# Filler products of one pass and 512 columns, and none in the stages with experts

## The reference

```python
def _L0_attn_ref(x, w_qkv, w_proj, b_proj):      # HEADS = 16, HEAD_SIZE = 8
    q, k, v = jnp.split(x @ w_qkv, 3, axis=-1)   # each to (batch, head, token, 8)
    wei = jnp.einsum('bhqd,bhkd->bhqk', q, k) * HEAD_SIZE ** (-0.5)
    wei = jax.nn.softmax(jnp.where(causal, wei, -jnp.inf), axis=-1)
    out = jnp.einsum('bhqk,bhkd->bhqd', wei, v)  # back to (batch, token, 128)
    return out @ w_proj + b_proj

def _L0_ffn_ref(x, Wg, W1, b1, W2, b2):          # 8 experts, 128 -> 512 -> 128
    topk_logits, topk_idx = jax.lax.top_k(xt @ Wg.T, 2)
    gates = zeros.at[rows, topk_idx].add(softmax(topk_logits))
    h = gelu(jnp.einsum('th,ehi->tei', xt, W1) + b1)
    o = jnp.einsum('tei,eih->teh', h, W2) + b2
    return jnp.einsum('te,teh->th', gates, o)

xn = _layernorm(x)
x = x + attn(xn) + ffn(xn)
```

## Time and profile before

| | |
|---|---|
| time before, median of 3 executions | 870.83 us (866.7 to 873.35) |
| the profiled execution, its own time | 874.43 us |
| its span, first to last instruction | 872.7 us |
| mean granted clock of TensorE | 0.842 |
| busy: PE, DVE, ACT, POOL | 740.8, 557.2, 449.5, 283.1 us |
| chain that ended last: PE, DVE, ACT, POOL | 64%, 19%, 3%, 2% |

### The profile page before, as it was taken

One profiled execution on the slowest core, in us unless ns is written; L12 is line 12 of the kernel. 1 busy time (PEld: TensorE's weight loads), 2 busy tenths in 40 slices (PEclk: granted clock), 3 DMA queues, 4 the chain that ended last, 5 costly groups with the idle time before them and its releaser, 6 DMA issues.

```text
span 872.7 us, 15135 instructions
## 1 busy us (share of the span) xinstructions
PE 740.8 (85%) x5021; PEld 420.3 (48%) x5021; DVE 557.2 (64%) x2164; ACT 449.5 (52%) x717; POOL 283.1 (32%) x454
## 2 busy tenths in 40 slices
PE   3683779986788989888898999889998989899995
PEld 2562434432345554544555555545545555555543
DVE  4749535554576666767667666756676766667656
ACT  2212123233355566655656665646566666666663
POOL 7103841573502333323132322222242323141421
PEclk9555555567797799999799989989799999898997
DMA  6997310210239051523425250605234342430074
GB/s 154 166 154 257 116 40 13 70 47 23 68 78 273 16 159 43 148 77 103 115 71 140 57 147 18 193 29 133 86 92 118 87 118 83 142 107 5 22 180 120
DMA packets 96261, 88.74 MB, mean 102 GB/s; under 512 B 8368, under 2 KB 83672, under 8 KB 96184
## 3 DMA queue, kind: packets, MB, share of 16 engines
q1 hardware_dynamic: 91432, 78.05, 34.6%
q0 software_dynamic: 4544, 9.35, 3.3%
q10 hardware_dynamic: 208, 0.38, 0.2%
HBM read 50.18 MB, written 21.32 MB: 82 GB/s over the span
## 4 chain that ended last, share of the span: by engine, by line
PE 64%; DVE 19%; issue 4%; SPq 4%; DMA 3%; ACT 3%; POOL 2%; another core or an unknown queue 2%; DVEq 0%; ACTq 0%; POOLq 0%
PE ov L773 18%; PE aux L741 15%; PE aux L831 10%; PE aux L783 6%; DVE maxes L963 5%; DVE junk L964 3%; SPq L444 3%; PE sc L695 3%; PE aux L788 2%; DMA hid<-in_L_ffn_W 2%; PE sc L696 2%; PE sc L697 2%; DVE maxes L959 2%; DVE xrow L1017 2%
## 5 line engine op out<-in xcount | busy, mean ns | idle before, releaser
L648 ACT ACTIVATE probs<-sc 128x1024 f32<-128x1024 f32 (+3 forms) x384 | 295.4, 810 | 254.5 <-PE sc L759 241.3
L741 PE MATMUL aux<-kT,qT 32*128 32x512 f32 (+3 forms) x768 | 244.6, 483 | 79.4 <-DVE maxes L964 22.6
L561 POOL TENSOR_SCALAR_AFFINE_SELECT probs<-probs 128x256 f32<-128x256 f32 x256 | 103.8, 409 | 422.7 <-ACT probs L648 418.7
L963 DVE TENSOR_REDUCE maxes<-aux 128x1 f32<-128x128 f32 (+2 forms) x384 | 161.1, 420 | 70.9 <-PE aux L741 64.3
L959 DVE TENSOR_REDUCE maxes<-aux 128x1 f32<-128x512 f32 x256 | 163.4, 684 | 60.1 <-PE aux L741 54.3
L741 PEld LDWEIGHTS aux<-kT,qT 32*128 32x128 f32 x768 | 108.3, 205 | 193.6 <-DVE maxes L964 52.7
L773 PE MATMUL ov<-probs,v 128*32 128x512 f32 (+3 forms) x1536 | 187.9, 565 | 2.4 <-POOL probs L561 2.3
L759 PE MATMUL sc<-qT,kT 32*128 32x512 f32 (+3 forms) x768 | 170.6, 465 | 4.2 <-DMA qT<-mT 2.7
L964 DVE CUSTOM_DVE_ANT_0 junk<-aux,cst 128x128 f32<-128x128 f32 x512 | 140.7, 282 | 19.3 <-PE aux L741 18.1
L586 POOL DMA_INDIRECT ys<-ysb,back x78 | 76.0, 974 | 77.4 <-issue 46.3
L831 PEld LDWEIGHTS aux<-w2b,hid 128*128 128x128 f32 x624 | 78.6, 197 | 41.8 <-DVE maxes L964 28.8
(11 more groups left out here) (117 smaller groups left out, 647.4 us busy)
## 6 DMA issues: line engine op xcount, KB each, us to landing
w1b<-w_scr SPq DMA_DIRECT2D x39, 512.0 KB, 4.3
w2b<-in_L_ffn_W SPq DMA_DIRECT2D x39, 256.0 KB, 3.5
xs<-ysb SPq DMA_DIRECT2D x6, 838.5 KB, 19.0
xrow<-in_L_attn_x SPq DMA_DIRECT2D x8, 512.0 KB, 6.6
kT<-kqh SPq DMA_DIRECT2D x32, 128.0 KB, 2.8
qT<-kqh SPq DMA_DIRECT2D x32, 128.0 KB, 2.7
w_scr<-w1b SPq DMA_DIRECT2D x8, 512.0 KB
xsin<-xs SPq DMA_DIRECT2D x9, 387.0 KB
```

What stands on the lines that cost most here:

```text
L561: nc.gpsimd.affine_select(out=block_, in_=block_, compare_op=ALU.is_ge, fill=0.0, base=0, pattern=[[0, 2], [1, P]], channel_multiplier=-1) ...
L648: nc.scalar.activation(probs[:, s % 2, 2 * half:2 * half + 2, 0:cols], pair(part)[:, :, 0:cols], ACT.Exp).then_inc(sc_done, 1)
L741: nc.tensor.matmul(bank(part)[:, 0:cols], qT[n % 3][rows, P * i:P * i + P], kT[n % 3][rows, k0:k0 + cols], start=True, stop=True).then_inc ...
L963: nc.vector.reduce_max(maxes[:, i, other, h:h + 1], bank(part)[:, 0:cols - P], axis=AX.X)
```

## The change

The fillers are four products of 512 columns in place of three of 128. The stationary operand is the first 128 columns of `wh`, the moving one 512 columns of `xh` in stages 0 to 2 and of `xsh` in stage 15 (`xh` is overwritten there by then); both are of the one-pass type. The groups stand only in stages without experts: the 22 of the stages 3 to 14 go, 35 remain, at the places where they were.

```diff
@@ -168,7 +168,7 @@
         group = take(count)
-        if not any(x[0] in full_array for x in parts[here:]):
+        if f is None and not any(x[0] in full_array for x in parts[here:]):
             parts.append(("warm", n, s))
@@ -245,7 +245,7 @@
-WARM = 3
+WARM = 4
@@ -779,8 +779,9 @@
                     unit = NEXT_AUX[part]
                     if unit:
                         aux_free(unit)
+                        moving = xh if part[1] < FFN_UNIT[0] else xsh
                         for _ in range(WARM):
-                            nc.tensor.matmul(bank(unit)[:, 0:P], ident, upper, start=True, stop=True)
+                            nc.tensor.matmul(bank(unit)[:, :], wh[:, 0:P], moving[:, 0:W], start=True, stop=True)
```

## The result

| | before | changed |
|---|---|---|
| median of 20 executions, us | 872.76 (866.7 to 878.86) | 878.91 (867.55 to 886.21) |
| profiled execution, its own time and span, us | 874.43, 872.7 | 874.78, 873.0 |
| mean granted clock | 0.842 | 0.839 |
| ratio to before, 95% interval | | 1.0057 (1.0031 to 1.0083) |

The change makes the kernel 0.6% slower, 5 us, where 20 us less were forecast. The ratio leaves out executions more than 1.5% above the fastest of their kernel, so it is nearer to 1 than the quotient of the medians.

What follows compares the result with a forecast made beforehand. PE was taken to bound the stages with experts, with DVE behind it. The terms gave 874.4 - 23.0 + 9.0 - 8.0 + 2.0 = 854.4 us for the profiled execution, 851 against the median, range 836 to 863.

Steps and rivals of the forecast that it cites:

- Where PE is the bound and the groups on the chain: Stages with experts, 283 to 831 us: PE busy 502.09 of 548 us, and the critical chain runs through the fillers.
- the work behind can move up by the whole of a group in both kinds of place: Steps 1 and 10, stages with experts: removing 22 groups frees 25.6 us, less a tenth for DVE, 23.0 gained.
- a sign of being wrong: At steps 1 and 10, what DVE waited for there turns into PE waiting for DVE; no size given.
- 2 us lost, with ends of 2 gained and 15 lost: Stages with experts: without groups the clock may come back later, three more spells of 3 us, partly offset.
- The last rival: Stages with experts: without groups at step 10 or 11 the clock falls more often; slower, 881 us; chance 0.05.
- the 64 us more at half that it asked for: Stages with experts: added half-clock time needed for the kernel to be slower by 1%, nearly double the present 77 us.
- The rule of short idles that I set against the change: Skill page: short idles between groups of products make the clock swing; groups at step 10 or 11 would hold it.
- The longer groups, 9 us: Stages 0 to 2 and 15: 35 groups each one product longer, 9 us lost; no less than 5, no more than 11.
- the clock of the early stages, 8 us gained: Stages 0 to 2: wide products bring the clock up more often, about a fifth of 43 us; ends 0 and 25.
- Stage 15: Only about six of its nine longer groups count, 1.4 us lost, since the chain leaves PE at about 848 us.
- The price of a us at half clock: Where PE is the bound, a us at half clock that turns full saves 0.45 us.

Runs made afterwards that it cites:

- the fit: Half-stage lengths in 15 traces, fitted with a price per us at half clock and per kind of group; three old products: 0.29 us at step 1, 0.50 at step 10.
- the first series: Four kernels beside the one before (858.7 us): only the removal 1.0055, only wide early fillers 1.0027, wide fillers at all 57 places 1.0034, no filler 0.9893.

## Why the prediction was wrong

**Where PE is the bound and the groups on the chain:** right as a reading, wrong as a proof. The chain has a group in full because it follows one releaser; it doesn't say when the next would have come.

**The step that failed: "the work behind can move up by the whole of a group in both kinds of place", 23.0 us gained.** By the fit it is 12 x 0.29 + 10 x 0.50 = 8.5 us. I took DVE's idle behind a group for proof that DVE stood ready. It only shows that DVE ran dry during the group. What counts is how long the others were still at work when the group began. At step 10 of stage 8 the group begins at 549.94, and DVE reads on until 550.46 before its idle:

```profile
550.18 0.28 DVE L964 CUSTOM_DVE_ANT_0 junk<-aux,cst 128x128 f32<-128x128 f32 x1
550.38 0.08 DVE L964 DVE_READ_ACCUMULATOR2_ANT maxes<- 128x1 f32 x1
```

That is 0.52 us of the group's 0.86 in which one of the three banks behind it, the third, was not free. The first bank was free, which I had checked; but three maxima stand behind the group, and the second pair of scores and the values behind the third. In the changed kernel, DVE and PE at the same place:

```profile
550.72 0.28 DVE L965 CUSTOM_DVE_ANT_0 junk<-aux,cst 128x128 f32<-128x128 f32 x1
550.92 0.08 DVE L965 DVE_READ_ACCUMULATOR2_ANT maxes<- 128x1 f32 x1
551.00 1.29 DVE L960 TENSOR_REDUCE maxes<-aux 128x1 f32<-128x512 f32 x2
```

```profile
549.48 1.06 PE L773 MATMUL ov<-probs,v 128*32 128x512 f32 x8
550.47 0.50 PE L741 MATMUL aux<-kT,qT 32*128 32x512 f32 x1
550.52 1.03 PE L741 MATMUL aux<-kT,qT 32*128 32x512 f32 x2
551.07 0.38 PE L759 MATMUL sc<-qT,kT 32*128 32x256 f32 x2
551.48 0.85 PE L773 MATMUL ov<-probs,v 128*32 128x384 f32 x8
```

DVE no longer idles, as I forecast, and PE waits for it instead, which the prediction had named as a sign of being wrong. The third maximum, alone in a window that starts later, begins only at 551.06, behind the read that ends at 551.00:

```profile
551.06 0.49 PE L741 MATMUL aux<-kT,qT 32*128 32x512 f32 x1
```

From values to values it is 2.00 us, where 548.94 to 551.35 before is 2.41. 0.41 us came of 0.86.

At step 1 it is ACT. Behind the experts' gelu it loads the table of the exponential and is behind by that. Stage 10, at half clock in both kernels; ACT before:

```profile
616.06 1.28 ACT L648 ACT_TABLE_LOAD   x1
617.35 1.94 ACT L648 ACTIVATE probs<-sc 128x1024 f32<-128x1024 f32 x2
```

and PE, before and changed:

```profile
617.96 1.65 PE L783 MATMUL aux<-cst 128*128 128x128 f32 x6 [0.34 <-DVE maxes L964]
619.54 0.79 PE L741 MATMUL aux<-kT,qT 32*128 32x512 f32 x1
619.54 0.69 PE L759 MATMUL sc<-qT,kT 32*128 32x384 f32 x2
619.55 1.11 PE L741 MATMUL aux<-kT,qT 32*128 32x512 f32 x2
620.13 0.52 PE L759 MATMUL sc<-qT,kT 32*128 32x384 f32 x2
620.59 1.94 PE L773 MATMUL ov<-probs,v 128*32 128x512 f32 x8
```

```profile
616.75 0.79 PE L741 MATMUL aux<-kT,qT 32*128 32x512 f32 x1 [0.34 <-DVE maxes L965]
617.22 0.69 PE L759 MATMUL sc<-qT,kT 32*128 32x384 f32 x2
617.42 1.66 PE L741 MATMUL aux<-kT,qT 32*128 32x512 f32 x2
618.30 0.68 PE L759 MATMUL sc<-qT,kT 32*128 32x384 f32 x2
619.01 1.93 PE L773 MATMUL ov<-probs,v 128*32 128x512 f32 x8
```

ACT's exponentials ended at 619.29, 1.33 us after the group began, and until then the second pair of scores has no bank of `sc`. By this reading the group of 1.58 us costs 0.25; the distance to the values shrank by 0.37, from 2.63 to 2.26 us. Behind the group the seven products of 32 rows ran close together: four of them start at 619.54 to 619.55, and the values follow 1.05 us later, at 620.59. Without the group they start one by one as their banks come free. The Trainium skill, "TensorE: Matmul & The Clock Gate", section "Why this matters for your kernels", says that products on different groups of 32 rows run side by side; the trace agrees, with the four that start within 0.01 us. I take this for the reason why waiting for all banks first costs PE little; no run shows it. At step 1 of the twelve stages ACT's exponentials end 0.79 to 1.34 us after a group's start and DVE's reads 0.62; at nine of the ten other places DVE's end 0.24 to 0.54 us after, at the last 0.82. What is left of the groups is 12 x 0.48 and 10 x 0.39, 9.7 us: near the fit's 8.5. This reading was to be had from the trace of before. That ACT is the cover at step 1 is read from these traces alone; no run took its table load away.

**The clock in the stages with experts, "2 us lost, with ends of 2 gained and 15 lost":** mis-sized. It is 34 us more at half clock at 0.35, 12 us, inside the bound that I kept and did not weigh. In stage 8 the spell was 518.7 to 525.4; in the changed kernel:

```profile
517.70:531.20 13.50, 13.42 (x67) 7.33 (x68) 6.50 (x27) 4.44 (x8) 4.26 (x9) 0.50 0.04 12
```

I had noted that the group at 519.80 did not prevent the spell. It lasts 13.5 us without it. So it is in the other stages: before there are twelve spells of 3.4 to 10.2 us, each beginning within 1.4 us of the group at step 1; in the changed kernel there are thirteen of 3.4 to 13.7. The spells became longer and hardly more frequent. The last rival had the clock right and the place wrong, and the 64 us more at half that it asked for were not needed: 34 were enough, because the removal gave 8.5 us and not 23. The groups at step 1 hold the clock, not those at step 10: with the first alone 82 us are at half, with both 72 to 92. The rule of short idles that I set against the change pointed the right way too, but that idles are the cause is not shown: in this spell PE is busy 13.42 of 13.50 us.

**The longer groups, 9 us, and the clock of the early stages, 8 us gained:** about right. A new group is 213.29 to 214.41, 1.12 us at full clock, and 159.06 to 160.93, 1.87 at half, where I had 1.09 and 2.01. In the first series the early stages had 19 us less at half, worth 6.8 at the 0.35 of the stages with experts, and the time stayed (197.7 and 196.8 us), so the longer groups cost about 7.7. Stage 15 cost 1.7 us in the profiled execution, 1.4 forecast.

**The price of a us at half clock:** 0.45, measured 0.32 to 0.35 in the stages with experts.

With 8.5 in place of 23.0 and 12 in place of 2 the sum is 874.4 - 8.5 + 9 - 8 + 12 = 879 us, 4.5 above the profiled execution of before, and the measured ratio is 5 us. That it comes so close is partly luck: the profiled execution of the changed kernel was 874.8 us, since its early stages were 3.6 us shorter than in the trace of before, where the first series has them 0.9 longer, and the stages with experts 2.8 longer, where the sum has 3.5.

## What to carry to other kernels

The idle of a neighbour behind a piece of work doesn't tell what removing the piece gives. Take the piece's start, look at every engine for which the next products wait, at each bank and not only at the first, and subtract what they still have to do; only the rest of the piece is to be had. Filler that is covered this way and holds the clock is cheap, and its first part is the cheapest: size it by the cover, and put none where little of it is covered and the clock stays down with it.

## What was not expected of the hardware

The clock did not need fillers that use the whole array: with products on 32 of its 128 columns the stages with experts had 82 us at half clock, with full ones 72 to 92, with none 109. Two products kept it as well as three (68 us in both traces, and 72 and 92), one did not (102). Why two and not one is left open.

Early fillers at half clock in stages 0 and 1 cost 1.2 us each, in a stretch where the clock stayed at half with them and without them. And the code of a stretch does not fix its clock: with their 22 groups of three the stages with experts had 72, 75, 75, 78, 78 and 92 us at half clock in six traces, for 548 to 556 us, and both ends belong to one kernel. What decides it is open.
